# A decoder kernel whose timetable for 884 maxima reckons with VectorE alone, and with VectorE and TensorE together

## The chip, the cores and the metric

The kernel runs on one core of a Trainium2 chip. Its time is the device time of one execution in microseconds (us). The smaller, the better.

## The reference, cut to what matters

A sequence of 1024 tokens with 128 features goes through three parts, each with a residual and a normalisation: four layers of a recurrent cell (sLSTM) with a small gated network behind each, a cross attention with 16 heads over 6404 context rows, and a layer of eight experts.

```python
def step(carry, wx_t):                      # the recurrent cell, 1024 steps, one after the other
    h, c, n, m = carry
    raw = wx_t + jnp.einsum('bhd,hdgo->bhgo', h, rk) + b
    ...
    hn = jax.nn.sigmoid(og) * cn / nn
    return ((hn, cn, nn, mn), hn)
...
scores = jnp.einsum('bqhd,bkhd->bhqk', q, k) * scale
attn = jax.nn.softmax(scores, axis=-1)      # needs the largest score of each query and head
out = jnp.einsum('bhqk,bkhd->bqhd', attn, v).reshape(B, Nq, h * dh)
```

## The kernel before

Each of the four layers is a recurrence over all 1024 tokens. The kernel runs the four as a skewed pipeline, each layer two chunks of 32 tokens behind the one before it: 38 chunks of 32 steps, 1216 steps in all. Each step is a closed ring. TensorE makes 16 small matmuls of the weights with the state (L1179), ScalarE four functions of the gates (L1079 to L1082), VectorE nine small instructions (L1290 to L1319), which end with the new state `st`, and only then can TensorE begin the next step. Beside the ring each chunk has its own work, spread by hand over its 32 steps (`beside`): normalisations, the convolution, the gated network, the gate matmuls for the next chunk. In what follows t is the place of a step in its chunk, 0 to 31.

The first 10 chunks (`chunks(0, FIRST)`) hold nothing else. From chunk 10 on (896 steps, numbered here from 0) part of the attention is laid into the gaps of the ring: 4 blocks of 128 queries with 4 units each (a unit is 4 heads of a block). A unit has 51 tiles of keys, and a unit begins every 52 steps, from step 64 on: in each step three score matmuls (L236 to L238), one value matmul in two passes (L1131) and one exponential on ScalarE (L1068).

The softmax of a unit needs the maxima of its scores beforehand. That is 52 pieces of work for each unit (13 slices of keys for 4 heads), each of one matmul of 128x512 into one of two banks (L245, `pe_max_score`, tile `MB`) and one reduction on VectorE that reads the bank (L253, `dve_max`). They are made during the unit before. With the maxima for one unit more there are 17 sets, 884 pieces. The class `Timetable` sets at build time in which steps they stand. For the maxima of a unit there is a window of 51 steps (fewer for the first two sets); every step in it gets a room, which is `ROOM` (1.15) less the step's entry in `vector_load` less a surcharge for special steps of the attention (`special`), and the 52 pieces are laid out in proportion to the running sum of the rooms. So a step gets none, one or two of them, in rare cases more.

Within a step the order on each engine is fixed. On TensorE: the 16 recurrence matmuls, scores, values, attention work with a bank, the maxima's matmuls, the chunk's matmuls. On VectorE: the nine instructions of the ring, the chunk's work, the attention's, the reductions. All run in that order, so a reduction stands ahead of the next step's L1290.

After step 895 the other 16 units run in a tail without the recurrence, and then the experts; neither is touched.

Of the kernel before, what the change touches and what calls it, by code (L numbers as in the profile page):

```python
# [38 lines left out]
class Attention:  # L39
# [9 lines left out]
    def __init__(self, nc, ctx, dims, blocks_inside):  # L49
        self.nc = nc  # L50
        S, D, HEADS, DHEAD, NK, DC = dims
        self.S, self.D, self.HEADS, self.DHEAD, self.NK, self.DC = dims
        self.TILES = S // P
        self.blocks_inside = blocks_inside
        self.KT = -(-NK // P)
        self.LAST = NK - (self.KT - 1) * P
        self.KEYS = [(i, min(i + 512, NK)) for i in range(0, NK, 512)]
        self.MX = self.HEADS_A_UNIT * len(self.KEYS)
        self.UNITS_A_BLOCK = HEADS // self.HEADS_A_UNIT
        KT, N, U4 = self.KT, self.N, self.UNITS_A_BLOCK  # L60

        def sb(name, shape, dt=F32):
            return ctx.enter_context(nc.sbuf_tensor(name, shape, dt))

        self.identa = sb("identa", [P, P])
        self.keys_h = sb("keys_h", [DC + 1, KT * P], F16)
        self.keys_l = sb("keys_l", [DC, KT * P], F16)
        self.vals = sb("vals", [P, KT, DC + 1])
        self.vals_c = sb("vals_c", [P, KT, 2 * DC + 1], F16)
        self.qk_w = sb("qk_w", [P, HEADS, DC])  # L70
        self.vo_w = sb("vo_w", [DC, HEADS, D])
        self.post_w = sb("post_w", [P, D])
        self.pick_den = sb("pick_den", [DC + 1, 1])
        self.ln_prob = sb("ln_prob", [P, 1])
        self.qh = sb("qh", [DC + 1, U4, N], F16)
        self.ql = sb("ql", [DC, U4, N], F16)
        self.xs = sb("xs", [P, D])
        self.xo = sb("xo", [P, D])
        self.xa = sb("xa", [P, D])
        self.xn_a = sb("xn_a", [P, D])  # L80
        self.xat = sb("xat", [P, P])
        self.sta = sb("sta", [P, 6])
        self.mva = sb("mva", [P, 2])
        self.vra = sb("vra", [P, 1])
        self.rsa = sb("rsa", [P, 1])
        self.neg_half = sb("neg_half", [P, 1])
        self.mx = sb("mx", [P, self.HEADS_A_UNIT, len(self.KEYS)])
        self.mxn = sb("mxn", [P, self.HEADS_A_UNIT])
        self.o_sb = sb("o_sb", [DC + 1, N])
        self.rden = sb("rden", [P, self.HEADS_A_UNIT])  # L90
        self.y_unit = sb("y_unit", [P, blocks_inside * U4 + 1, D])
# [251 lines left out]
class Timetable:  # L343
# [2 lines left out]
    ROOM = 1.15  # L346
    MAX_COST = 0.667

    def __init__(self, at, blocks, steps, chunk_steps, vector_load):
        period, units = at.KT + 1, blocks * at.UNITS_A_BLOCK  # L350
        start = [2 * chunk_steps + period * u for u in range(units + 2)]
        assert start[units] <= steps
        self.units = units
        self.scores = {start[u] + i: (u, i) for u in range(units) for i in range(at.KT)}
        self.values = {s + 1: tile for s, tile in self.scores.items()}
        self.keep = {start[u] + at.KT: u for u in range(units)}
        self.out = {start[u] + period: u for u in range(units - 1)}
        self.block = {24: 0}
        self.block.update({start[at.UNITS_A_BLOCK * b - 2] - 13: b for b in range(1, blocks + 1)})
        self.turn = {s + 9: b for s, b in self.block.items()}  # L360
        self.queries = {35: 0, 46: 1}
        self.queries.update({start[v - 2] - 1: v for v in range(2, units + 2)})
        self.column = {start[v] - 4: v for v in range(units + 1)}
        self.row = {start[v] - 3: v for v in range(units + 1)}
        asked = {v: s for s, v in self.queries.items()}
        special = {s: 1.3 for s in self.out}
        special.update({s: 0.6 for s in self.column})
        for s in self.queries:
            special[s + 2] = special.get(s + 2, 0.0) + 0.7
        for s in self.block:  # L370
            for i in range(9):
                special[s + i] = special.get(s + i, 0.0) + 0.35
        self.maxes = {}
        for v in range(units + 1):
            window = range(max(asked[v] + 2, start[v] - period - 3), start[v] - 4)
            room = [max(0.02, self.ROOM - vector_load[s % chunk_steps] - special.get(s, 0.0)) for s in window]
            total, so_far, n = sum(room), 0.0, 0
            for s, r in zip(window, room):
                so_far += r
                upto = at.MX if s == window[-1] else min(at.MX, int(so_far / total * at.MX + 0.5))  # L380
                if upto > n:
                    self.maxes.setdefault(s, []).extend((v, i) for i in range(n, upto))
                n = upto
        self.uses, free, count = {}, [-1.0, -1.0], [0, 0]

        def take(key, read_at):
            bank = 0 if free[0] <= free[1] else 1
            self.uses[key] = (bank, count[bank])
            free[bank] = read_at
            count[bank] += 1  # L390

        for s in range(steps):
            if s in self.out:
                take(("den", self.out[s]), s + 0.5)
                take(("out", self.out[s]), s + 0.6)
            if s in self.turn:
                take(("turn", self.turn[s]), s + 1.3)
            if s in self.queries:
                take(("queries", self.queries[s]), s + 2.5)
            if s in self.row:  # L400
                take(("row", self.row[s]), s + 1.3)
            for i, key in enumerate(self.maxes.get(s, ())):
                take(("max",) + key, s + 0.7 + 0.01 * i)
        self.block_step = {}
        for s, b in self.block.items():
            for after, step in ((0, 0), (1, 1), (3, 4), (4, 5), (5, 6), (6, 7), (6, 8), (8, 11)):
                self.block_step.setdefault(s + after, []).append((b, step))
        self.scale = {s + 1: (b, 1) for s, b in self.block.items()}
        self.scale.update({s + 6: (b, 2) for s, b in self.block.items()})
        ends = {b: s + 12 for s, b in self.block.items()}  # L410
        self.load = {max(4 * b, -(-ends.get(b - 1, 0) // chunk_steps)): b for b in ends}
        self.store = {ends[b] // chunk_steps: b for b in ends}
        assert len(self.load) == len(self.store) == len(ends)


def slstm_stage(nc, x, w, scratch_in, scratch_out, dims, at, first_row, xa_out):
# [7 lines left out]
    CH = P // L  # L424
# [3 lines left out]
    ITERS = NCH + LAG * (L - 1)  # L428
# [6 lines left out]
    FIRST, KT = 10, at.KT  # L435
# [3 lines left out]
    with ExitStack() as ctx:  # L439
# [530 lines left out]
        def chunks(base, count, plan=None):  # L970


            with nc.Block() as block:
# [217 lines left out]
                def _(dve):  # L1191
# [90 lines left out]
                    for p in range(count):  # L1282
# [44 lines left out]
            nc.gpsimd.sem_clear(range(nums[0], nums[0] + len(nums)))  # L1327
            nc.all_engine_barrier()

        vector_load = [0.4, 0.4, 0.4, 0.4, 0.6, 0.3, 0.6, 0.9, 0, 0.1, 0.4, 0.6, 0.7, 0.7, 0.35, 0.7, 0.1, 0.5, 0.35, 0.32,  # L1330
                       0.5, 0.6, 0.4, 1.2, 1.2, 0.6, 0.6, 0.5, 0.15, 0.15, 0.15, 0.3]
        chunks(0, FIRST)
        chunks(FIRST, ITERS - FIRST, Timetable(at, at.blocks_inside, (ITERS - FIRST) * CH, CH, vector_load))


        with nc.Block() as block:
# [659 lines left out]
```

## Time and profile before

| | |
|---|---|
| runs | 4732.89, 4746.34, 4748.07 us, median 4746.34 |
| profiled execution | 4731.98 us, span of its instructions 4730.3 us |
| busy over the span | PE 82%, PE weight loads 49%, DVE 73%, ACT 62%, POOL 17% |
| recurrence alone (10 chunks) | from 125.3 to 879.4 us |
| recurrence with attention, steps 0 to 895 | from 879.4 to 3239 us |
| attention tail and experts | from 3239 us on |

The profiled execution lies at the low end of the three runs. A time of one step is read as the distance between the starts of its first ScalarE instruction (L1079) and of the next step's.

### The profile page before, as it was taken

What the parts mean: (1) busy time and instruction counts of PE and PEld (TensorE: products, weight loads), DVE (VectorE), ACT (ScalarE), POOL (GpSimd) and SP (SyncE); (2) the same over time, 40 slices, a digit from 0 to 9 for tenths busy, and PEclk for the clock granted to TensorE, in tenths of its full rate; (3) what the DMA queues carried; (4) which work ended last, traced back from release to release, by engine and by line L of the source; (5) the groups of instructions that cost most, each with busy time, mean ns of one, the idle gap of its engine ahead of it and who ended that gap; (6) DMA issues with size and microseconds to landing.
All of it is one profiled execution on the core that took longest, in us unless ns stands there. A gap on an engine that the chain in (4) does not pass through costs nothing. (4 is left out here: it accounts for less than half of the span.)

```text
span 4730.3 us, 104841 instructions
## 1 busy us (share of the span) xinstructions
PE 3893.7 (82%) x38546; PEld 2305.6 (49%) x38546; DVE 3450.6 (73%) x15547; ACT 2928.5 (62%) x9151; POOL 800.6 (17%) x998
## 2 busy tenths in 40 slices
PE   3343434469999999999999999998999999999959
PEld 2332323334454544445444454544666666666636
DVE  4666666788888888888888888886665657666441
ACT  1444444436666666666666666666887878888812
POOL 1000000000000000000000000002554545555500
PEclk7555555559999999999999999998999999999969
DMA  2000000000000000000000000000000000000020
GB/s 61 2 3 3 2 3 2 4 2 2 4 3 3 3 2 4 4 3 2 2 4 3 3 2 3 3 2 3 2 1 3 2 3 2 1 1 1 1 59 5
DMA packets 34825, 26.11 MB, mean 6 GB/s; under 512 B 9453, under 2 KB 32677, under 8 KB 34278
## 3 DMA queue, kind: packets, MB, share of 16 engines
q1 hardware_dynamic: 34310, 19.37, 1.6%
q8 instruction: 308, 5.05, 0.4%
q14 instruction: 207, 1.70, 0.1%
HBM read 15.27 MB, written 2.88 MB: 4 GB/s over the span
## 5 line engine op out<-in xcount | busy, mean ns | idle before, releaser
L1179 PE MATMUL G<-st,rec_w 128*128 128x1 f16 x19456 | 683.1, 165 | 550.2 <-DVE st L1319 532.9
L1179 PEld LDWEIGHTS G<-st,rec_w 128*128 128x128 f16 x19456 | 605.1, 99 | 1006.0 <-DVE st L1319 974.4
L1131 PE MATMUL OA<-pf,vals 128*97 128x512 f32 (+1 forms) x1632 | 849.4, 601 | 0.6
L1500 POOL TENSOR_TENSOR plt<-pft,pht 128x512 f16<-128x512 f32 x544 | 634.9, 1168 | 565.6 <-ACT pft L1495 563.1
L253 DVE TENSOR_REDUCE mx<-MT 128x1 f32<-128x512 f32 x780 | 508.7, 667 | 253.8 <-PE MT L245 248.7
L1088 ACT ACTIVATE st<-hb 32x16 f16<-32x16 f32 x1216 | 259.0, 213 | 696.7 <-DVE hb L1314 696.0
L1493 ACT ACTIVATE pht<-ST,ln_prob 128x512 f16<-128x512 f32 (+1 forms) x816 | 560.5, 687 | 200.4 <-PE ST L238 140.4
L253 DVE TENSOR_REDUCE mx<-MB 128x1 f32<-128x512 f32 (+1 forms) x884 | 571.0, 660 | 41.4 <-PE MB L245 25.9
L1068 ACT ACTIVATE pf<-SC,ln_prob 128x512 f32<-128x512 f32 (+1 forms) x816 | 560.5, 687 | 20.8
L1495 ACT ACTIVATE pft<-ST,ln_prob 128x512 f32<-128x512 f32 (+1 forms) x816 | 554.2, 679 | 0.0
L1079 ACT ACTIVATE tf<-G 32x16 f32<-32x16 f32 x1216 | 211.7, 174 | 483.8 <-PE G L1179 465.4
L1290 DVE SCALAR_TENSOR_TENSOR uu<-tf,cn 32x32 f32<-32x32 f32 x1216 | 214.6, 176 | 295.9 <-ACT tf L1079 287.1
L1561 PE MATMUL OT<-vals_c,pht 128*128 128x193 f16 (+1 forms) x3264 | 409.1, 248 | 7.0 <-DVE o_n L1586 6.4
L245 PE MATMUL MB<-keys_h,qh 96*128 96x512 f16 (+1 forms) x884 | 319.0, 386 | 29.5 <-DVE mx L253 24.5
L1131 PEld LDWEIGHTS OA<-pf,vals 128*97 128x97 f32 (+1 forms) x1632 | 269.3, 167 | 148.3 <-issue 11.7
L1561 PEld LDWEIGHTS OT<-vals_c,pht 128*128 128x128 f16 (+1 forms) x3264 | 288.4, 98 | 98.9 <-issue 17.5
L236 PE MATMUL ST<-qh,keys_l 96*128 96x512 f16 (+1 forms) x816 | 314.3, 385 | 18.9 <-issue 12.2
L1570 PEld LDWEIGHTS OT<-vals_c,plt 128*128 128x128 f16 (+1 forms) x3264 | 228.3, 97 | 202.1 <-issue 13.5
L1296 DVE RECIPROCAL rn<-cn 32x16 f32<-32x16 f32 x1216 | 292.9, 241 | 41.9
L238 PE MATMUL SC<-qh,keys_h 97*128 97x512 f16 (+1 forms) x816 | 314.7, 386 | 0.0
L237 PE MATMUL SC<-ql,keys_h 96*128 96x512 f16 (+1 forms) x816 | 313.0, 384 | 0.0
L238 PE MATMUL ST<-qh,keys_h 97*128 97x512 f16 (+1 forms) x816 | 312.9, 384 | 0.0
(293 smaller groups left out, 6410.4 us busy)
## 6 DMA issues: line engine op xcount, KB each, us to landing
w<-in_L_ffn_W SPq DMA_DIRECT2D x16, 256.0 KB, 5.9
xin<-x SPq DMA_DIRECT2D x38, 48.0 KB, 1.8
rnat<-in_L_attn_rker SPq DMA_DIRECT2D x3, 256.0 KB, 4.2
up_w<-in_L_attn_ff_up SPq DMA_DIRECT2D x1, 672.0 KB
scr_out<-x SPq DMA_DIRECT2D x39, 16.0 KB, 1.6
xin<-scr_in SPq DMA_DIRECT2D x38, 16.0 KB, 1.7
wq_sb<-in_L_xattn_Wq SPq DMA_DIRECT2D x1, 512.0 KB, 3.7
wo_sb<-in_L_xattn_Wo SPq DMA_DIRECT2D x1, 512.0 KB, 8.6
```

Of the source, the lines that this page charges most:

```text
L236: pe.matmul(bank[0:k, :], at.keys_l[:, keys], at.qh[0:DC, unit, :], start=True, stop=False)
L237: pe.matmul(bank[0:k, :], at.keys_h[0:DC, keys], at.ql[:, unit, :], start=False, stop=False)
L238: return pe.matmul(bank[0:k, :], at.keys_h[:, keys], at.qh[:, unit, :], start=False, stop=True)
L245: return pe.matmul(bank[:, 0:a1 - a0], at.qh[0:at.DC, unit, i * P:(i + 1) * P], at.keys_h[0:at.DC, a0:a1], start=True, stop=True)
L253: return at.nc.vector.tensor_reduce(at.mx[:, i, c:c + 1], bank[:, 0:a1 - a0], AX_X, ALU.max)
L1068: s.activation(pf[0:rows, tile % 2, :], SC[tile % 2][0:rows, :], ACT.Exp, scale=1.0 / at.S_SCALE, bias=at.ln_prob[0:rows, 0:1]).then_inc(p ...
L1131: pe.matmul(OA[0:at.DC + 1, :], at.vals[0:rows, i, :], pf[0:rows, tile % 2, :], start=(i == 0), stop=(i == KT - 1)).then_inc(pv_done, 1)
L1179: mm = pe.matmul(g[:, t, c:c + 1], rec_w[:, c, :], st[:, c:c + 1], start=False, stop=(c == C - 1), skip_group_check=True)
L1493: s.activation(ph[0:k, t % NP_, :], SC[t % NS][0:k, :], ACT.Exp, scale=1.0 / at.S_SCALE, bias=at.ln_prob[0:k, 0:1])
L1495: s.activation(pf[0:k, t % NP_, :], SC[t % NS][0:k, :], ACT.Exp, scale=1.0 / at.S_SCALE, bias=at.ln_prob[0:k, 0:1]).then_inc(p_done, 1)
L1500: return eng.tensor_tensor(pl[0:k, t % NP_, :], pf[0:k, t % NP_, :], ph[0:k, t % NP_, :], ALU.subtract)
L1561: pe.matmul(OA[i // 2][:, (i % 2) * 256:(i % 2) * 256 + VC], ph[0:k, t % NP_, i * P:(i + 1) * P], at.vals_c[0:k, j, :], start=(j == 0 and ...
```

## The change

The room of a step is now reduced by a second list too, `tensor_load`, with an entry for each t at which the chunk has matmuls. The entries of `vector_load` at several of those t become smaller, and the least room is 0 instead of 0.02.

```diff
@@ -346,7 +346,7 @@
-    def __init__(self, at, blocks, steps, chunk_steps, vector_load):
+    def __init__(self, at, blocks, steps, chunk_steps, vector_load, tensor_load):
@@ -373,7 +373,8 @@
-            room = [max(0.02, self.ROOM - vector_load[s % chunk_steps] - special.get(s, 0.0)) for s in window]
+            room = [max(0.0, self.ROOM - vector_load[s % chunk_steps] - tensor_load[s % chunk_steps] - special.get(s, 0.0))
+                    for s in window]
@@ -1327,10 +1328,12 @@
-        vector_load = [0.4, 0.4, 0.4, 0.4, 0.6, 0.3, 0.6, 0.9, 0, 0.1, 0.4, 0.6, 0.7, 0.7, 0.35, 0.7, 0.1, 0.5, 0.35, 0.32,
...
+        tensor_load = [0, 0, 0, 0, 0, 0, 0, 0, 0, 0.4, 0.7, 0, 0, 0.3, 0, 0, 0.5, 0.6, 0, 0,
...
```

No instruction is added or removed, 884 pieces stay 884; only their steps change. From step 64 to 891 there are 828 pieces in both kernels. Before, 133 of these 828 steps hold two of them and 133 none; now 170 hold two or more (two of these hold three, steps 328 and 744) and 172 none. By t the number of steps with two or more, and with none, in these 828 steps:

| t | two or more: before, now | none: before, now |
|---|---|---|
| 0 | 7, 5 | 3, 3 |
| 1 | 4, 10 | 2, 4 |
| 2 | 4, 12 | 2, 0 |
| 3 | 4, 8 | 0, 0 |
| 5 | 6, 16 | 2, 0 |
| 7 | 0, 0 | 11, 14 |
| 8 | 15, 22 | 4, 4 |
| 9 | 18, 10 | 2, 2 |
| 10 | 1, 0 | 0, 4 |
| 13 | 0, 0 | 8, 23 |
| 14 | 4, 16 | 0, 0 |
| 16 | 9, 4 | 4, 4 |
| 18 | 11, 4 | 0, 0 |
| 19 | 4, 19 | 0, 0 |
| 26 | 0, 0 | 0, 17 |
| 28 | 15, 10 | 3, 3 |
| 29 | 8, 7 | 2, 2 |
| 30 | 19, 20 | 0, 0 |

The other places change by two steps or less in either column.

Three places show the moves. First VectorE in step 173 (t = 13) and step 174 (t = 14), before: from the reduction of step 173 (`mx`) over the nine instructions of the ring and one of the chunk's (`gq`) to the reduction of step 174.

```order
L253 TENSOR_REDUCE mx<-MB 128x1
L1290 SCALAR_TENSOR_TENSOR uu<-tf,cn 32x32
L1293 SCALAR_TENSOR_TENSOR cn<-ei,uu 32x16
L1296 RECIPROCAL rn<-cn 32x16
L1298 SCALAR_TENSOR_TENSOR vv<-ei,tz 32x16
L1302 SCALAR_TENSOR_TENSOR ww<-to,rn 32x16
L1312 TENSOR_TENSOR cn<-uu,vv 32x16
L1314 SCALAR_TENSOR_TENSOR hb<-ww,cn 32x16
L1316 SCALAR_TENSOR_TENSOR st<-ww,cn 32x16
L1319 TENSOR_TENSOR st<-hb,st 32x16
L886 SCALAR_TENSOR_TENSOR gq<-gq,TP 128x168
L253 TENSOR_REDUCE mx<-MB 128x1
```

The same place now, from the chunk's last work of step 173 on (line numbers behind the diff are one higher).

```order
L887 SCALAR_TENSOR_TENSOR gq<-gq,gs 128x168 x2
L1291 SCALAR_TENSOR_TENSOR uu<-tf,cn 32x32
L1294 SCALAR_TENSOR_TENSOR cn<-ei,uu 32x16
L1297 RECIPROCAL rn<-cn 32x16
L1299 SCALAR_TENSOR_TENSOR vv<-ei,tz 32x16
L1303 SCALAR_TENSOR_TENSOR ww<-to,rn 32x16
L1313 TENSOR_TENSOR cn<-uu,vv 32x16
L1315 SCALAR_TENSOR_TENSOR hb<-ww,cn 32x16
L1317 SCALAR_TENSOR_TENSOR st<-ww,cn 32x16
L1320 TENSOR_TENSOR st<-hb,st 32x16
L887 SCALAR_TENSOR_TENSOR gq<-gq,TP 128x168
L253 TENSOR_REDUCE mx<-MB 128x1 x2
```

The reduction of step 173 has gone behind that of step 174: t = 13 has none, t = 14 has two, and L1291 of step 175 stands behind both.

Second VectorE in step 179 (t = 19), before: from the ring's last instruction over two of the chunk's small ones (`pw`, `ke`) and the reduction to the start of step 180.

```order
L1319 TENSOR_TENSOR st<-hb,st 32x16
L1258 TENSOR_SCALAR pw<-nlo 32x16
L1260 TENSOR_SCALAR ke<-nlo 32x16
L253 TENSOR_REDUCE mx<-MB 128x1
L1290 SCALAR_TENSOR_TENSOR uu<-tf,cn 32x32
L1293 SCALAR_TENSOR_TENSOR cn<-ei,uu 32x16
```

The same place now.

```order
L1320 TENSOR_TENSOR st<-hb,st 32x16
L1259 TENSOR_SCALAR pw<-nlo 32x16
L1261 TENSOR_SCALAR ke<-nlo 32x16
L253 TENSOR_REDUCE mx<-MB 128x1 x2
L1291 SCALAR_TENSOR_TENSOR uu<-tf,cn 32x32
L1294 SCALAR_TENSOR_TENSOR cn<-ei,uu 32x16
```

One reduction has become two in this step; step 178 has one instead of two.

Third TensorE in step 186 (t = 26), before: recurrence, scores, values, a maximum's matmul (`MB`), and three gate matmuls of the chunk.

```order
L1179 MATMUL G<-st,rec_w 128x1 x16
L236 MATMUL SC<-qh,keys_l 128x512
L237 MATMUL SC<-ql,keys_h 128x512
L238 MATMUL SC<-qh,keys_h 128x512
L1131 MATMUL OA<-pf,vals 97x512
L245 MATMUL MB<-keys_h,qh 128x512
L828 MATMUL G<-gx,gate_w 128x32 x3
```

The same place now.

```order
L1180 MATMUL G<-st,rec_w 128x1 x16
L236 MATMUL SC<-qh,keys_l 128x512
L237 MATMUL SC<-ql,keys_h 128x512
L238 MATMUL SC<-qh,keys_h 128x512
L1132 MATMUL OA<-pf,vals 97x512
L829 MATMUL G<-gx,gate_w 128x32 x3
```

The maximum's matmul is gone from this step, and with it the reduction on VectorE.

## Rows read from the trace of the kernel before

The columns of Rows 1 are: window, its length, busy time of each engine with the number of its instructions, the granted TensorE clock as a share of 2.4 GHz, the DMA share. Step numbers and t are as above.

**Rows 1.** Windows: steps 32 to 63; steps 64 on; two unit boundaries.
```profile
core 0: us, PE busy (x) PEld busy (x) DVE busy (x) ACT busy (x) POOL busy (x), PEclk, DMA share, GB/s
954.70:1061.60 106.90, 63.35 (x664) 36.20 (x665) 86.97 (x396) 34.82 (x177) 3.44 (x10) 0.50 0.01 3
1061.60:3239.30 2177.70, 2070.41 (x20303) 1062.64 (x20302) 1871.10 (x9692) 1434.26 (x5325) 96.08 (x276) 0.98 0.01 3
1330.70:1346.00 15.30, 15.03 (x117) 9.20 (x116) 9.34 (x49) 7.63 (x28) 1.11 (x4) 0.67 0.00 1
2425.50:2438.30 12.80, 12.34 (x116) 6.79 (x115) 9.27 (x48) 7.55 (x27) 1.11 (x4) 0.87 0.01 1
```

**Rows 2.** Groups by shape, 1061.6 to 3239.3 us: busy us, mean ns, idle before.
```profile
L253 DVE TENSOR_REDUCE mx<-MB 128x1 f32<-128x512 f32 x764 | 509.8, 680 | 35.5 <-PE MB L245 21.5
...
L245 PE MATMUL MB<-keys_h,qh 96*128 96x512 f16 x764 | 271.5, 380 | 3.9 <-DVE mx L253 3.9
```

**Rows 3.** Timeline of an ordinary step, all engines: start us, length us, instruction.
```profile
1904.97 0.17 ACT L1079 ACTIVATE tf<-G 32x16 f32<-32x16 f32 x1
...
1906.25 0.38 PE L245 MATMUL MB<-keys_h,qh 96*128 96x512 f16 x1
...
1906.43 0.17 DVE L1319 TENSOR_TENSOR st<-hb,st 32x16 f16<-32x16 f32 x1
...
1906.66 0.55 PE L1179 MATMUL G<-st,rec_w 128*128 128x1 f16 x16
1906.91 0.69 DVE L253 TENSOR_REDUCE mx<-MB 128x1 f32<-128x512 f32 x1
...
1907.30 0.17 ACT L1079 ACTIVATE tf<-G 32x16 f32<-32x16 f32 x1
...
1907.52 0.17 DVE L1290 SCALAR_TENSOR_TENSOR uu<-tf,cn 32x32 f32<-32x32 f32 x1
```

**Rows 4.** ScalarE timeline, first instruction of steps 110, 111, 112.
```profile
1177.97 0.17 ACT L1079 ACTIVATE tf<-G 32x16 f32<-32x16 f32 x1
...
1180.63 0.17 ACT L1079 ACTIVATE tf<-G 32x16 f32<-32x16 f32 x1
...
1182.95 0.17 ACT L1079 ACTIVATE tf<-G 32x16 f32<-32x16 f32 x1
```

**Rows 5.** The same of steps 142, 143, 144.
```profile
1266.10 0.17 ACT L1079 ACTIVATE tf<-G 32x16 f32<-32x16 f32 x1
...
1268.42 0.17 ACT L1079 ACTIVATE tf<-G 32x16 f32<-32x16 f32 x1
...
1271.31 0.17 ACT L1079 ACTIVATE tf<-G 32x16 f32<-32x16 f32 x1
```

**Rows 6.** The same of steps 147 and 148.
```profile
1279.06 0.17 ACT L1079 ACTIVATE tf<-G 32x16 f32<-32x16 f32 x1
...
1281.87 0.17 ACT L1079 ACTIVATE tf<-G 32x16 f32<-32x16 f32 x1
```

**Rows 7.** The same of steps 358 and 359.
```profile
1832.41 0.17 ACT L1079 ACTIVATE tf<-G 32x16 f32<-32x16 f32 x1
...
1835.24 0.17 ACT L1079 ACTIVATE tf<-G 32x16 f32<-32x16 f32 x1
```

**Rows 8.** The same of steps 92 and 93.
```profile
1132.25 0.17 ACT L1079 ACTIVATE tf<-G 32x16 f32<-32x16 f32 x1 [0.23 <-PE G L1179]
...
1135.18 0.17 ACT L1079 ACTIVATE tf<-G 32x16 f32<-32x16 f32 x1 [0.63 <-PE G L1179]
```

**Rows 9.** The same of steps 316 and 317.
```profile
1720.90 0.17 ACT L1079 ACTIVATE tf<-G 32x16 f32<-32x16 f32 x1 [0.23 <-PE G L1179]
...
1723.61 0.17 ACT L1079 ACTIVATE tf<-G 32x16 f32<-32x16 f32 x1 [0.42 <-PE G L1179]
```

**Rows 10.** Timeline of step 122 (t = 26), VectorE and TensorE.
```profile
1215.46 0.16 DVE L1319 TENSOR_TENSOR st<-hb,st 32x16 f16<-32x16 f32 x1
...
1215.73 0.54 PE L1179 MATMUL G<-st,rec_w 128*128 128x1 f16 x16
```

More of the change, by code:

```diff
@@ L1328, in chunks @@
             nc.all_engine_barrier()
-        vector_load = [0.4, 0.4, 0.4, 0.4, 0.6, 0.3, 0.6, 0.9, 0, 0.1, 0.4, 0.6, 0.7, 0.7, 0.35, 0.7, 0.1, 0.5, 0.35, 0.32,
-                       0.5, 0.6, 0.4, 1.2, 1.2, 0.6, 0.6, 0.5, 0.15, 0.15, 0.15, 0.3]
+        vector_load = [0.4, 0.4, 0.4, 0.4, 0.6, 0.3, 0.6, 0.9, 0, 0, 0, 0.6, 0.7, 0.7, 0.35, 0.7, 0, 0.16, 0.35, 0.32,
+                       0.5, 0.6, 0.32, 1.2, 1.2, 0.6, 0.5, 0.35, 0, 0, 0, 0.2]
+        tensor_load = [0, 0, 0, 0, 0, 0, 0, 0, 0, 0.4, 0.7, 0, 0, 0.3, 0, 0, 0.5, 0.6, 0, 0,
+                       0, 0, 0.3, 0, 0, 0, 0.35, 0.35, 0.4, 0.35, 0.35, 0.25]
         chunks(0, FIRST)
-        chunks(FIRST, ITERS - FIRST, Timetable(at, at.blocks_inside, (ITERS - FIRST) * CH, CH, vector_load))
+        chunks(FIRST, ITERS - FIRST, Timetable(at, at.blocks_inside, (ITERS - FIRST) * CH, CH, vector_load, tensor_load))
         with nc.Block() as block:
```

## The prediction

> **What bounds the kernel now.** I read the windows by stage first. From step 64 to the end of the recurrence there are 2177.7 us for 832 steps, 2.62 us each, with TensorE busy for 2070 us (95%), VectorE for 1871 us (86%) and ScalarE for 1434 us (66%) [rows 1]. This is the stretch in which most maxima move; 52 of the 884 pieces are made in steps 32 to 63, of 106.9 us [rows 1]. Before step 32, in the tail and in the experts nothing changes.
>
> A busy share does not tell what a step costs, since the step is a ring. So I took the timeline of one plain step, 385 [rows 3]. It goes from 1904.97 to 1907.30, 2.33 us. At 1906.25 the matmul of its one maximum starts (0.38 us, so until 1906.63); at 1906.43 VectorE starts the last instruction of the ring, until 1906.60; at 1906.66 TensorE begins the next recurrence. Both inputs of that start, the engine and the state, are there within 0.03 us of each other. Behind the ring VectorE then runs the reduction, 1906.91 to 1907.60, and the next step's L1290 starts at 1907.52, when its input from ScalarE (1907.30 + 0.17) has just come. So one maximum in a plain step is free on both engines. Step 111 with one maximum reads 2.32 us too [rows 4], and I found no step of this stretch below that.
>
> What a second maximum costs has two parts that fall on different steps. Its matmul stands ahead of the next recurrence in its own step. Its reduction stands ahead of the next step's L1290, so it lengthens the **next** step. Each counts only as far as its engine is the later one: the two lengthen a step by the greater, not by the sum.
>
> **Prices, by pairs of equal places in the trace of before.** The distance of the first ScalarE instructions of two steps is the length of a step; n is the number of maxima.
> - VectorE, behind a step with two, place lightly loaded: step 147 follows one with two and takes 1281.87 - 1279.06 = 2.81 us [rows 6], against 2.32: +0.49. Step 359 begins 2.83 us after 358, which follows a pair at t = 5 [rows 7]: +0.51. Step 143 follows a pair at t = 14: 1271.31 - 1268.42 = 2.89, against step 111 behind a single: 1182.95 - 1180.63 = 2.32 [rows 4, 5]: +0.57.
> - At t = 1, 2, 3 the chunk's own VectorE work already fills the step; there nothing is free and I take 0.60 for a further reduction, near its whole length, 0.68 us [rows 2].
> - VectorE, behind a step with none: step 142 (none before it, two in it) takes 1268.42 - 1266.10 = 2.32 us, step 110 (one, one) 1180.63 - 1177.97 = 2.66 [rows 4, 5]: -0.34 for t = 14.
> - TensorE: step 92 (t = 28) with two takes 1135.18 - 1132.25 = 2.93 us [rows 8], step 316 with one 1723.61 - 1720.90 = 2.71 [rows 9]: 0.22 for a maximum in a step that TensorE fills. In step 142 two maxima in a plain step cost nothing at all, so there TensorE has this 0.22 to spare.
> - t = 26, the place with the most removals: VectorE's last ring instruction ends at 1215.46 + 0.16 = 1215.62, the recurrence starts at 1215.73 [rows 10], 0.11 us later, against 0.06 in the plain step (1906.66 - 1906.60 [rows 3]). So VectorE is only about 0.05 us behind TensorE. Taking TensorE's 0.22 away gives 0.05, because the step then waits for VectorE.
>
> **The sum, steps 64 to 891,** with the counts of the table of places:
> - more steps with two: t = 1, 2, 3: +18 at 0.60 = +10.8; t = 5: +10 at 0.51 = +5.1; t = 14: +12 at 0.57 = +6.8; t = 19: +15 at 0.49 = +7.4; t = 20, 21, 25: +5 at 0.5 = +2.5; t = 8: +7. The step behind it (t = 9) had a pair in front in 15 cases already and is partly filled by TensorE; between 0 and 0.5 I take 0.25, the middle, = +1.8. Sum +34.4.
> - fewer steps with two: t = 18: -7 at 0.49 = -3.4; t = 0: -2 at 0.60 = -1.2; t = 28 and 29: -6 at 0.22 = -1.3; t = 22: -2 at 0.4 = -0.8. t = 9 and 16, -13: the steps behind (t = 10, 17) have chunk matmuls and are filled by TensorE anyway, so 0. Sum -6.7.
> - more steps with none: t = 13: +15 at -0.34 = -5.1; t = 26: +17 at -0.05 = -0.9; t = 7: +3 at about -0.45 = -1.4; t = 10 and 17, where TensorE is the later: +6 at -0.22 = -1.3. Those at other places that lose or gain one nearly cancel: 0. Sum -8.7.
> - special steps and steps 32 to 63 (step 47 goes from one to three, step 48 from two to none), and the third maximum in steps 328 and 744: between -3 and +4, taken as +1.
>
> Together 34.4 - 6.7 - 8.7 + 1 = **+20 us**, all from VectorE. The bounds: with every added pair at 0.4 and the removals at full TensorE price (t = 26: -3.7) it is +9; with every added pair at the whole reduction, 0.68, it is +31. The sum stands against the profiled execution, 4731.98 us, and gives 4752. That execution lies 14 us (0.3%) below the median of the runs, 4746.34; I put the same 20 us on the median: 4766, and say **4765 us**, +0.4%. A difference under 0.3% (14 us) can't be told from no change here: the runs shown spread over 15.
>
> **A rule against a row.** In this stretch TensorE's matmul time fills 95% [rows 1], which would make it the engine to relieve. The weight loads fill 1062.6 of 2177.7 us, 49%, and VectorE 86% [rows 1]. The Trainium skill (Perfetto Trace Analysis, Identifying the Most-Contended Engine) says that matmul busy time is not a good measure and that one goes by weight loads on Tensor and by occupancy elsewhere, and relieves the fullest engine first. By that rule VectorE is the one, and a change that makes pairs of reductions to spare TensorE goes the wrong way; by matmul busy time it would go the right way, which is the first rival. The sum above needs neither.
>
> **Rivals.**
> 1. *TensorE is the later one nearly everywhere, faster.* For it: 95% busy, and in the plain step its matmul ends 0.03 us behind VectorE's state. Then added reductions are hidden and each maximum that leaves a step with chunk matmuls gives 0.22. From t = 9, 10, 13, 16, 17, 22 and 26 to 31 together 68 leave (t = 26 alone 17): -15 us, 4731. It decides if the steps behind the new pairs stay at 2.3 to 2.4. Against it: steps 143, 147 and 358 [rows 5, 6, 7], the very pairs that become many. Chance 0.05.
> 2. *The added pairs cost about half,* because a step that is late on VectorE catches up in the next, or the special steps gain: +9, 4755, within 0.3%. For it: the last reduction of each row of 13 is shorter, and unit boundaries lose some maxima right ahead of their long VectorE work (steps 167, 425, 583 and 841). Against it: the lengths read above are from start to start, so a catching up would show in them; step 142 and the steps after it are not shorter than 2.32. Chance 0.20.
> 3. *The clock.* The two unit boundaries of the same steps (168 and 584) take 15.3 us at a mean clock of 0.67 and 12.8 us at 0.87 [rows 1]: 2.5 us for some 7 us more at the lower level, 1.2 GHz. 12 of 15 boundaries have such a stretch. If the steps without maxima bring one to each boundary and to as many places again, that is 15 x 2.5 = +38 on top, 4785 or more; if they only shift, +-6. Against it: at t = 26 and 13 TensorE keeps over 80% of its work. The Trainium skill (TensorE: Matmul & The Clock Gate, Part 1) says that idleness of TensorE lowers the clock and activity restores it; here the row agrees so far that the lower level stands at the boundaries, where no scores run. Chance 0.04.
> 4. *The change doesn't do what it says.* In part it doesn't: steps at t = 28 to 30 with two go from 42 to 37 only. As the numbers are laid out in proportion, a lower room for a few places raises the share of all others. If the moves cancel throughout: 4746. Chance 0.03.
>
> **Chances and range.** Forecast (+14 us or more) 0.68, its own range 4757 to 4778; rivals as above. Slower by over 0.3%: 0.68 + 0.04 = 0.72. Within: 0.20 + 0.03 = 0.23. Faster: 0.05. The range must take in the half price (4755), the upper bound of the sum (+31, 4777) and that the runs themselves lie between 4733 and 4748: 4747 to 4781.
>
> **What would show it.** In the profile after: the stretch from step 64 to 895 takes 2197 instead of 2177.7 us; steps behind a pair at t = 2, 5, 14, 19 read 2.8 to 3.1 us; steps at t = 14 behind none read 2.32; steps at t = 26 without a maximum 2.63 instead of 2.68 (2.46 would speak for rival 1); L1079's idle time behind TensorE changes little, and that of L1179 behind `st` grows by about the 20 us. I am wrong if the steps behind the new pairs don't grow, if the price at t = 26 is 0.2, or if the boundaries change by more than 5 us together.

## The result and the profile after

The changed kernel takes 4756.56 us in the median of 14 runs (4752.18 to 4758.34), the kernel before 4746.51 us in the median of 14 runs (4731.36 to 4756.77). The medians stand 10 us apart. The ratio is 1.0024, 95% interval 1.0015 to 1.0034: slower by 11 us, 7 to 16. That interval covers the scatter of the runs, not the clock's part between two programs, which the last experiment puts at some 10 us; that the change itself costs time rests on the steps, read below. The direction is the forecast's, the size about half of it, and below the 14 us that the prediction called the least to be told apart. The profiled execution took 4758.22 us, its span is 4756.5 us, 26.2 more than before. The pages of both read alike; here the page of the kernel after.

```profile
span 4756.5 us, 104841 instructions
...
PE 3902.9 (82%) x38546; PEld 2310.9 (49%) x38546; DVE 3450.4 (73%) x15547; ACT 2928.4 (62%) x9151; POOL 800.6 (17%) x998
```

No engine has more or less to do. The windows of the kernel after for steps 32 to 63, for steps 64 on, and for the seven steps 270 to 276 around a unit boundary (columns as in [rows 1]):

```profile
core 0: us, PE busy (x) PEld busy (x) DVE busy (x) ACT busy (x) POOL busy (x), PEclk, DMA share, GB/s
955.30:1061.20 105.90, 63.03 (x664) 36.02 (x665) 87.02 (x396) 34.84 (x178) 3.44 (x10) 0.50 0.01 3
1061.20:3262.20 2201.00, 2079.07 (x20303) 1068.14 (x20302) 1871.22 (x9692) 1434.20 (x5325) 96.32 (x276) 0.98 0.01 3
1604.80:1628.30 23.50, 22.53 (x193) 11.78 (x192) 16.84 (x85) 12.98 (x48) 0.08 (x1) 0.78 0.04 10
```

Steps 64 on take 23.3 us more than in [rows 1], steps 32 to 63 1.0 less. The same seven steps in the kernel before:

```profile
1602.80:1621.60 18.80, 17.98 (x191) 9.94 (x190) 15.76 (x84) 12.94 (x47) 0.06 (x1) 1.00 0.05 13
```

They took 4.7 us less there, at a full clock; after, the mean clock is 0.78. So part of the 23 us is the clock and not the timetable. To separate the two I added up, in both profiles, the lengths of the same 655 steps away from the unit boundaries (of steps 64 to 891 all but those from three before a unit's start to seven behind it; a length is again the distance of two first ScalarE instructions). No half clock stands in them in either profile, and the 349 of them whose own and preceding number of maxima are the same differ by 0.2 us in sum. They take **11.4 us** more. The boundary steps take 12.0 us more, of which 2.7 stand in steps whose own or preceding number changed; the rest, 9.3, is mainly clock: 12 of the 15 boundaries had a stretch at half clock before, 78 us in all, and all 15 have one after, 99 us. (Among the boundary steps at full clock in both profiles, the changed ones take 2.1 us more and the others 0.4.) The tail, where nothing changed, took 3.2 us more, and the start of step 0 was 0.6 later. So 11.4 + 2.7 - 1.0 = 13.1 us belong to the places, and 9.3 + 3.2 + 0.6 = 13.1 to this pair of executions.

Where they stand is seen step by step. Steps 173, 174, 175 of the place shown first in the change (ScalarE's timeline after, first instruction of steps 174, 175, 176; those of before are shown with the last experiment):

```profile
1353.22 0.17 ACT L1080 ACTIVATE tf<-G 32x16 f32<-32x16 f32 x1
...
1355.54 0.17 ACT L1080 ACTIVATE tf<-G 32x16 f32<-32x16 f32 x1
...
1358.43 0.17 ACT L1080 ACTIVATE tf<-G 32x16 f32<-32x16 f32 x1
```

Step 174, with two maxima and none before it, takes 2.32 us (before 2.66), step 175 behind the pair 2.89 (before 2.32). Step 180, behind the new pair at t = 19 (steps 180 and 181 start at):

```profile
1368.47 0.17 ACT L1080 ACTIVATE tf<-G 32x16 f32<-32x16 f32 x1
...
1371.00 0.17 ACT L1080 ACTIVATE tf<-G 32x16 f32<-32x16 f32 x1
```

2.53 us instead of 2.32. One reduction of this pair is short: the last slice of each head has 260 columns, and its reduction takes 416 ns instead of 680 (kernel before, group by shape):

```profile
L253 DVE TENSOR_REDUCE mx<-MB 128x1 f32<-128x260 f32 x64 | 26.6, 416 | 0.5
```

Of the 13 steps away from the boundaries that stand behind a new pair at t = 19, the nine with two full reductions in front grew by 0.48 us each, the four with a short one by 0.21; together 5.1 us. And step 186 (t = 26), which has lost its maximum (steps 186 and 187 start at):

```profile
1382.78 0.17 ACT L1080 ACTIVATE tf<-G 32x16 f32<-32x16 f32 x1
...
1385.46 0.17 ACT L1080 ACTIVATE tf<-G 32x16 f32<-32x16 f32 x1
```

2.68 us, as long as before. TensorE has less to do and nothing is gained. The groups by shape say the same of the whole stretch; first after, then the kernel before:

```profile
L253 DVE TENSOR_REDUCE mx<-MB 128x1 f32<-128x512 f32 x764 | 507.9, 680 | 35.0 <-PE MB L245 20.6
L1180 PE MATMUL G<-st,rec_w 128*128 128x1 f16 x13296 | 457.7, 164 | 106.4 <-DVE st L1320 95.9
```

```profile
L1179 PE MATMUL G<-st,rec_w 128*128 128x1 f16 x13296 | 457.5, 164 | 92.7 <-DVE st L1319 79.6
```

TensorE's wait for the new state ahead of its recurrence has grown from 79.6 to 95.9 us.

One place has a price that the prediction did not have. Three steps before a unit's start, TensorE also writes the row of maxima (L263) into one of the two banks, so a second maximum in that step is the third use of two banks. Step 425 in the kernel before, with two maxima:

```profile
2007.80 0.39 PE L245 MATMUL MB<-keys_h,qh 96*128 96x512 f16 x1
...
2008.22 0.69 DVE L253 TENSOR_REDUCE mx<-MB 128x1 f32<-128x512 f32 x1 [1.15 <-PE MB L245]
...
2008.97 0.39 PE L245 MATMUL MB<-keys_h,qh 96*128 96x512 f16 x1 [0.79 <-DVE mx L253]
```

The second matmul waits until the first reduction has freed its bank, and the next recurrence stands behind it. The step takes 4.43 us with two maxima and 3.26 with one (after). The same 1.18 us are lost or gained wherever the count of such a step went between one and two: steps 425, 477 and 841 lost their second maximum, 165 and 581 got one.

### The profile page after: what moved, and what is told of

It reads as the page before. It is cut to its first block and busy times, and to the rows that moved or that the text cites. A ratio compares the mean times of both kernels' runs of the same rounds, so it can differ in the third digit from the quotient of the medians.

```text
span 4756.5 us, 104841 instructions
## 1 busy us (share of the span) xinstructions
PE 3902.9 (82%) x38546; PEld 2310.9 (49%) x38546; DVE 3450.4 (73%) x15547; ACT 2928.4 (62%) x9151; POOL 800.6 (17%) x998
## 3 DMA queue, kind: packets, MB, share of 16 engines
HBM read 15.27 MB, written 2.88 MB: 4 GB/s over the span
## 5 line engine op out<-in xcount | busy, mean ns | idle before, releaser
L1291 DVE SCALAR_TENSOR_TENSOR uu<-tf,cn 32x32 f32<-32x32 f32 x1216 | 214.6, 177 | 316.2 <-ACT tf L1080 308.6
```

## The experiments

The theory: a pair of maxima costs by VectorE in the next step, unless TensorE's chunk matmuls fill that step anyway. Rival A: TensorE is the later engine, its relief is what counts. Rival B: the difference of the two kernels comes from the clock at the unit boundaries. The table gives the ratio to the kernel before in runs on the same chip, and the difference to the profile of before: in the 655 steps away from the boundaries, in steps 32 to 63, and in the boundary steps whose own or preceding number of maxima changed and that stand at full clock in both profiles. The last three columns together are what the places cost.

| kernel | ratio, 95% interval | 655 steps, us | steps 32 to 63, us | changed boundary steps, us |
|---|---|---|---|---|
| the change | 1.0024 (1.0015 to 1.0034) | +11.4 | -1.0 | +2.1 |
| e1_vector_list_alone | 0.9992 (0.9983 to 1.0001) | -7.0 | +2.7 | -0.9 |
| e2_tensor_list_alone | 1.0072 (1.0058 to 1.0086) | +29.7 | +2.5 | +7.3 |
| e3_short_reduce_before | 0.9835 (0.9822 to 0.9848) | -60.7 | -11.2 | none changed |
| e4_short_reduce_after | 0.9814 (0.9801 to 0.9827) | -6.3 to e3 | -0.8 to e3 | -2.2 to e3 |
| e5_priced | 0.9942 (0.9927 to 0.9957) | -21.5 | -1.9 | +1.5 |
| e6_fill_before | 1.0000 (0.9989 to 1.0011) | -0.1 | 0.0 | none changed |
| e7_fill_after | 1.0046 (1.0030 to 1.0062) | +11.4 to e6 | -1.0 to e6 | +3.0 to e6 |
| e8_fill_out_only_before | 0.9993 (0.9982 to 1.0005) | +0.1 | 0.0 | none changed |
| e9_max_room | 1.0008 (0.9997 to 1.0018) | +6.9 | +1.0 | +2.0 |
| e10_only_13_to_14 | 0.9984 (0.9973 to 0.9996) | +2.5 | 0.0 | +0.2 |

**The two halves of the change.** First the new list for VectorE alone:

```diff
-        tensor_load = [0, 0, 0, 0, 0, 0, 0, 0, 0, 0.4, 0.7, 0, 0, 0.3, 0, 0, 0.5, 0.6, 0, 0,
-                       0, 0, 0.3, 0, 0, 0, 0.35, 0.35, 0.4, 0.35, 0.35, 0.25]
+        tensor_load = [0] * 32
```

> The new vector_load, tensor_load all zeros. The smaller entries stand at steps with chunk matmuls, so pairs gather there: 160 steps of two (133 before), with t = 9, 10, 16, 17 at 21, 12, 15, 13 (before 18, 1, 9, 0), t = 0 to 5 at 11 (before 25), t = 18 at 0 (before 11), and t = 7, 12 without a maximum in 19 and 13 (before 11, 8). Price theory (a pair costs 0.5 to 0.6 us where VectorE is the later engine in the next step, 0 to 0.25 where TensorE fills it): -14 x 0.6 - 11 x 0.49 for pairs gone, +11 x 0.22 (t = 10), +13 x 0.5 (t = 17), +6 x 0.45 (t = 27), +10 x 0.22 (t = 29 to 31), +4 x 0.4 (t = 22), zeros at t = 7, 12, 13, 11, 15 -7.5: about -5 us against the kernel before, in any case at or below it. Rival (TensorE is the later engine, so pairs in steps with chunk matmuls are what costs): slower than before by some 10 us.

Measured 4737.93 us against 4741.58, -4 us, an interval that just takes in no change; in its places -7.0, +2.7 and -0.9, together -5.2, as forecast. Then the new list for TensorE with the old one for VectorE:

```diff
-        vector_load = [0.4, 0.4, 0.4, 0.4, 0.6, 0.3, 0.6, 0.9, 0, 0, 0, 0.6, 0.7, 0.7, 0.35, 0.7, 0, 0.16, 0.35, 0.32,
-                       0.5, 0.6, 0.32, 1.2, 1.2, 0.6, 0.5, 0.35, 0, 0, 0, 0.2]
+        vector_load = [0.4, 0.4, 0.4, 0.4, 0.6, 0.3, 0.6, 0.9, 0, 0.1, 0.4, 0.6, 0.7, 0.7, 0.35, 0.7, 0.1, 0.5, 0.35, 0.32,
+                       0.5, 0.6, 0.4, 1.2, 1.2, 0.6, 0.6, 0.5, 0.15, 0.15, 0.15, 0.3]
```

> The old vector_load with the new tensor_load: the same idea, stronger. 202 steps of two or more (8 of them three and more), 54 of them at t = 0 to 4 (before 19), t = 5: 17 (6), t = 6: 5 (0), t = 20: 15 (0); t = 28 to 30 20 (42); none at t = 10, 13, 17, 26, 27 in 22, 21, 24, 19, 7 steps (0, 8, 4, 0, 2). Price theory: pairs at t = 0 to 4 +35 x 0.57, t = 5 and 6 +8.5, t = 11 +3, t = 14 +6, t = 18 to 20 +16, threes +5; TensorE relief -22 x 0.22 - 22 x 0.22 - 20 x 0.19 - 13 x 0.3 - 2: about +37 us against before, clearly slower than the change. Rival (TensorE the later one): about 100 maxima away from chunk matmuls at 0.22: 20 us faster than before.

4775.45 against 4741.58 us, +34; in its places +39.5 where +37 was forecast. The loss of the change sits in its TensorE list. Its VectorE list alone gives a little back by the places; the runs alone don't show that. Rival A had both signs wrong.

**VectorE's price taken away.** In both timetables the reductions of 16 of the 17 sets read 64 columns:

```diff
-    return at.nc.vector.tensor_reduce(at.mx[:, i, c:c + 1], bank[:, 0:a1 - a0], AX_X, ALU.max)
+    return at.nc.vector.tensor_reduce(at.mx[:, i, c:c + 1], bank[:, 0:columns or a1 - a0], AX_X, ALU.max)
...
-                            dve_max(at, MB[bank], i).then_inc(mb_read[bank], 1)
+                            dve_max(at, MB[bank], i, 64 if u < plan.units else None).then_inc(mb_read[bank], 1)
```

> The timetable of before; the reductions of the 16 sets for units beside the recurrence read 64 columns of the bank instead of 512, so those maxima are over part of the scores. Takes most of VectorE's price away and leaves TensorE's. Price theory: all single maxima that cost 0.1 to 0.47 at t = 2 to 8, 11 to 15 become free (some 2.3 us a chunk, 60 us), the 60 pairs outside TensorE's steps lose 0.5 each (30 us), unit boundaries some 10: about -100 us. Rival (TensorE the later one nearly everywhere): less than -30 us.

> The changed timetable with the same short reductions (maxima of the same 16 sets over part of the scores). Read against e3_short_reduce_before. Price theory: with VectorE's price gone only TensorE's terms are left, t = 26 now at its full 0.22 (-17 x 0.22), t = 28, 29 (-6 x 0.22), t = 10, 17 (-6 x 0.22): about -6 us against it, where the same two timetables with full reductions stand +13 us apart by their places. Rivals: if the difference of the two kernels came from the clock or from bank waits it stays at +10 or more.

4661.26 and 4653.52 us: -80 us to the kernel before (the expectation's 100 was too much: 60.7 and 11.2 us stand in the 655 steps and in steps 32 to 63, and the boundaries gave 2 in all instead of some 10), and the changed timetable is now the **faster** one by 8 us, where its slowest run (4653.95) lies below e3's fastest (4659.27). A short reduction takes 215 ns (group of e3, by shape) and not 680:

```profile
L253 DVE TENSOR_REDUCE mx<-MB 128x1 f32<-128x64 f32 x776 | 162.6, 215 | 41.3 <-PE MB L245 23.9
```

The windows from step 64 on, e3 and then e4:

```profile
1049.80:3164.70 2114.90, 2067.53 (x20303) 1065.50 (x20302) 1560.28 (x9692) 1437.00 (x5325) 96.02 (x276) 0.98 0.01 3
```

```profile
1049.80:3158.80 2109.00, 2058.59 (x20303) 1064.16 (x20301) 1558.91 (x9692) 1434.22 (x5324) 96.02 (x276) 0.98 0.01 3
```

And step 186 (t = 26), in e3 with its maximum and in e4 without (first instructions of steps 186 and 187):

```profile
1357.21 0.17 ACT L1079 ACTIVATE tf<-G 32x16 f32<-32x16 f32 x1
...
1359.88 0.18 ACT L1079 ACTIVATE tf<-G 32x16 f32<-32x16 f32 x1 [0.37 <-PE G L1179]
```

```profile
1356.63 0.17 ACT L1080 ACTIVATE tf<-G 32x16 f32<-32x16 f32 x1
...
1359.08 0.17 ACT L1080 ACTIVATE tf<-G 32x16 f32<-32x16 f32 x1
```

2.67 us with it, 2.45 without: the 0.22 us of TensorE are there, and with full reductions VectorE hides them. Away from the boundaries 11 steps at t = 26 lost their maximum and got no pair in front; they take 0.22 us less each here, and 0.00 less with full reductions. This pair settles the cause: same moves, opposite sign (-9.3 us in the places against +12.5), and only the length of the reduction differs. It speaks against rival B as well, since no half clock stands in the 655 steps.

**A timetable by prices.** The lengths of steps before give each t a price for its first and its second maximum; the 52 cheapest offers of a window are taken.

```diff
+            prices = []
+            for s in window:
+                first, second = first_price[s % chunk_steps], second_price[s % chunk_steps]
+                more = min(0.66, special.get(s, 0.0))
+                prices += [(first + more, s), (max(first, second) + more, s), (0.7 + more, s)]
...
+            chosen = sorted(s for _, s in sorted(prices)[:at.MX])
...
+        first_price = [0.01, 0.01, 0.1, 0.14, 0.25, 0, 0.2, 0.47, 0.08, 0, 0.22, 0.25, 0.34, 0.33, 0, 0.14, 0, 0.17, 0, 0,
+                       0.12, 0, 0, 0.6, 0.6, 0, 0, 0.2, 0.22, 0.22, 0.22, 0.3]
+        second_price = [0.6, 0.6, 0.6, 0.6, 0.6, 0.5, 0.6, 0.66, 0.2, 0.03, 0.23, 0.66, 0.66, 0.66, 0.56, 0.66, 0.05, 0.5, 0.45, 0.45,
+                         0.6, 0.5, 0.41, 0.66, 0.66, 0.6, 0.5, 0.45, 0.22, 0.22, 0.22, 0.4]
```

> A timetable by the measured prices: each step of a window offers a first and a second maximum at a price by t (first_price, second_price, read from the lengths of steps before; a surcharge for special steps as before), and the 52 cheapest offers are taken. Pairs at t = 0 to 5: 0 (before 25), t = 14, 18, 19: 6 (19), t = 8, 9, 16: 68 (42), t = 10: 26 (1), t = 28 to 30: 64 (42); none at t = 7, 12, 13 in 26, 20, 16 steps (11, 8, 8). Price theory, against before: -25 x 0.57 - 4 x 0.55 - 9 x 0.45 for dear pairs gone, +25 x 0.23 (t = 10) + 22 x 0.22 (t = 28 to 30) + 3 for other pairs, -15 x 0.47 - 12 x 0.34 - 8 x 0.33 - 2 for the maxima taken away: about -22 us, 0.5% faster than before. Rival (the later engine is TensorE; room by both loads together is right): it has more pairs in TensorE's steps than any kernel so far and should be slower than before by 10 us or more.

4716.41 us against 4744.26: ratio 0.9942, -28 us, faster than both kernels. In its places -21.5, -1.9 and +1.5: -22 as forecast. From step 64 on:

```profile
1060.80:3219.50 2158.70, 2073.08 (x20303) 1062.65 (x20301) 1872.62 (x9692) 1436.97 (x5324) 96.84 (x276) 0.98 0.01 3
```

Steps 200 to 202 (t = 8, 9, 10) in it, and then in the kernel before (first instructions of steps 200 to 203). The priced one has 0, 2, 2 and 2 maxima in steps 199 to 202, the other 1, 1, 2 and 1.

```profile
1414.07 0.17 ACT L1082 ACTIVATE tf<-G 32x16 f32<-32x16 f32 x1
...
1416.39 0.17 ACT L1082 ACTIVATE tf<-G 32x16 f32<-32x16 f32 x1
...
1419.08 0.17 ACT L1082 ACTIVATE tf<-G 32x16 f32<-32x16 f32 x1
...
1422.07 0.17 ACT L1082 ACTIVATE tf<-G 32x16 f32<-32x16 f32 x1 [0.38 <-PE G L1182]
```

```profile
1419.04 0.17 ACT L1079 ACTIVATE tf<-G 32x16 f32<-32x16 f32 x1
...
1421.84 0.17 ACT L1079 ACTIVATE tf<-G 32x16 f32<-32x16 f32 x1
...
1424.24 0.17 ACT L1079 ACTIVATE tf<-G 32x16 f32<-32x16 f32 x1
...
1427.08 0.17 ACT L1079 ACTIVATE tf<-G 32x16 f32<-32x16 f32 x1 [0.25 <-PE G L1179]
```

2.32, 2.69 and 2.99 us against 2.80, 2.40 and 2.84. The three steps take 8.00 against 8.04 us, though the four hold one maximum more: leaving t = 7 empty gives 0.48 in step 200, and the two pairs more cost 0.29 and 0.15.

**Greater load in place of the sum.**

```diff
-            room = [max(0.0, self.ROOM - vector_load[s % chunk_steps] - tensor_load[s % chunk_steps] - special.get(s, 0.0))
+            room = [max(0.0, self.ROOM - max(vector_load[s % chunk_steps], tensor_load[s % chunk_steps]) - special.get(s, 0.0))
```

> The change with one word other: room = 1.15 - max(vector_load, tensor_load) - special instead of the sum of both. Asks if it is the adding of the loads that costs. 142 steps of two (change 170). Pairs against before: t = 1 to 3 +11, t = 19, 20, 22 +19, t = 25 to 27 +13, t = 31 +13, t = 28 to 30 -23, t = 9 and 16 -15 (free ones), t = 0 and 18 -7. Price theory: +6 for t = 1 to 3, +9 for 19 to 22, +6 for 25 to 27, +4 for t = 31, -5 for 28 to 30, -4 for 0 and 18, +1 for t = 7, -2 for 10 and 17: about +16 us against before in its places, no better than the change, since any room by load moves pairs away from TensorE's steps where they are cheap. Rival (the adding is the fault, the greater load would be right): same as before or faster.

4746.35 against 4744.19 us, no difference to be measured in the runs; +6.9, +1.0 and +2.0 in its places, together +9.9, where I had expected +16. The change has +12.5 by the same count (13.1 with the boundary steps at half clock). So by the places the greater load still loses most of what the sum loses, and the adding is the smaller part of the fault. Some of the gap to the forecast is that 15 of its new pairs away from the boundaries hold a short reduction; the rest was not followed up.

**The clock at the unit boundaries.** Four matmuls more in the first score step of each unit and in its last step:

```diff
+                    def fill(bank, u):
+                        for _ in range(4):
+                            pe.matmul(bank[:, :], at.keys_l[:, 0:P], at.qh[0:at.DC, u % at.UNITS_A_BLOCK, :], start=True, stop=True)
...
+                        if i == 0 and u:
+                            fill(SC[tile % 2], u)
...
+                            if plan and n in plan.keep:
+                                tile = (plan.keep[n] + 1) * KT
+                                pe.wait_ge(p_done, tile - 1)
+                                fill(SC[tile % 2], plan.keep[n])
```

> The kernel before with four idle matmuls of 128x512 more (results overwritten) in the first score step of each unit from the second on and in the last step of each unit, which has no scores. Asks for the clock: the half clock stands at these unit boundaries (78 us in all, 12 of 15 boundaries in the profile of before). If TensorE's want of work there lowers the clock, the filling keeps it up: -28 us for the clock (2.5 us for 7), +19 for the matmuls themselves (0.87 us each in the last step, half hidden in the first): about -9 us. If the filling does not reach the clock: +19 us and the same stretches at half clock.

> The changed kernel with the same filling. Against e6_fill_before: if part of what the two profiles differ by (26 us) is the clock at the boundaries and the filling steadies it, only the places' price is left, +13 us. If the filling does not reach the clock: between +5 and +26, as the clock falls.

> The kernel before with the four matmuls only in the first score step of a unit. The first half-clock instructions stand there or one to two steps behind it. If that is late enough to hold the clock: -28 + 6 = some -20 us; if the want of work lies before it (score tiles of four rows and the last step): about +6 us with the half-clock stretches as before.

The filling reaches the clock: in e6 4 boundaries have half-clock stretches, 24 us in all, not 12 with 78. The granted clock of the runs agrees, 0.8745 in the median of e6's 12 and 0.867 in that of 24 runs of the kernel before. In e8 there are 8 with 68 us, so the matmuls of the first score step alone do little for the clock: neither of e8's two expectations came true. Steps 166 to 171 (a boundary), the kernel before and then e6:

```profile
1327.90:1348.00 20.10, 19.78 (x159) 11.30 (x158) 13.73 (x72) 11.82 (x42) 1.29 (x5) 0.75 0.00 1
```

```profile
1328.60:1347.10 18.50, 17.25 (x168) 9.38 (x167) 13.85 (x72) 11.85 (x43) 1.27 (x5) 1.00 0.01 1
```

1.6 us less with eight matmuls more. Over all it balances, where -9 had been expected: e6 4744.58 us against 4744.26; the interval of e8 (4740.61) takes in no change too. e6 ran 71 us less at half clock than the kernel before; at 0.39 us each (worked out with the last experiment) that is the forecast 28 us, so by this estimate the matmuls took about 28 and not 19. e7, the change with the same filling, took 4770.20 us, 26 more than e6 and not 13. In its profile the 655 steps are again 11.4 us above e6, exactly as in the unfilled pair, and the boundary steps 12.7; one boundary, around step 636, had 20.5 us at half clock in a row and alone was 9.5 us longer. e8 had the same 20.5 us at the same steps. In the runs e7 stood 30 us longer at half clock than e6 (granted clock 0.872 and 0.8745), about 12 us by the same estimate, which with the 13 of the places gives the 26. So the places' price came out clean and equal twice, but the filling did not make the two kernels' clocks equal, and why that stretch is so long stays open.

**One kind of move alone.**

```diff
+        for s in range(2 * chunk_steps + 13, steps, chunk_steps):
+            moved = self.maxes.get(s, [])
+            if len(moved) == 1 and len(self.maxes.get(s + 1, [])) == 1 and moved[0][0] == self.maxes[s + 1][0][0]:
+                self.maxes[s + 1] = self.maxes.pop(s) + self.maxes[s + 1]
```

> The kernel before with one kind of move alone: 18 single maxima of t = 13 go into the next step, which then holds two. Price theory: the step at t = 14 loses 0.34, the one at t = 15 gains 0.57, two of the moves stand at a unit boundary and count nothing: 16 x 0.23 = +4 us, in the profile at t = 15 +9 and at t = 14 -5, t = 13 unchanged. Rival (TensorE the later one; t = 13 has a chunk matmul): -18 x 0.22 = -4 us, at t = 13.

Starts of steps 173 to 176, the kernel before, then e10:

```profile
1350.59 0.17 ACT L1079 ACTIVATE tf<-G 32x16 f32<-32x16 f32 x1
...
1353.25 0.17 ACT L1079 ACTIVATE tf<-G 32x16 f32<-32x16 f32 x1
...
1355.91 0.17 ACT L1079 ACTIVATE tf<-G 32x16 f32<-32x16 f32 x1
...
1358.23 0.17 ACT L1079 ACTIVATE tf<-G 32x16 f32<-32x16 f32 x1
```

```profile
1350.32 0.18 ACT L1083 ACTIVATE tf<-G 32x16 f32<-32x16 f32 x1
...
1352.97 0.17 ACT L1083 ACTIVATE tf<-G 32x16 f32<-32x16 f32 x1
...
1355.30 0.17 ACT L1083 ACTIVATE tf<-G 32x16 f32<-32x16 f32 x1
...
1358.17 0.17 ACT L1083 ACTIVATE tf<-G 32x16 f32<-32x16 f32 x1
```

2.66, 2.66, 2.32 us before; 2.65, 2.33, 2.87 in e10. Summed away from the boundaries: t = 13 0.0, t = 14 -3.6, t = 15 +6.3, all other t within 0.2: +2.5 us, of the +4 expected. (14 of the 18 moves stand away from the boundaries; 8 of them cost 0.56 at t = 15, and 6 that hold a short reduction 0.30.) The steps do what the theory says. But the runs say 4737.48 against 4744.19 us, -7 us, and no step that the move touches is behind that.

The granted clock of the runs is. It has a median of 0.870 in e10 and 0.867 in the 23 runs of the kernel before beside it. Twice the missing share times the run's time is the time at half clock: 1232 and 1262 us, 30 less. Over those 23 runs of one and the same kernel the time rises by 0.36 us for each us at half clock (correlation 0.94; over the 24 runs beside e6 0.39 and 0.93). So the clock is worth about -11 us and the places +3, an estimate of -8, where -7 was measured. The runs alone don't tell a difference of a few us in the timetable; read beside their clocks they fit the places in this case and in e7.

## Why the prediction was right, and where its sizes were off

- *The mechanism* (the pair's reduction stands ahead of the next step's L1290): right. Steps 174, 175 and 180 read about as forecast, e3 and e4 turn the sign round with the reduction's length alone, e10 shows one kind of move by itself.
- *The prices* held away from the boundaries. Steps behind a new pair of full reductions grew by 0.51 us at t = 6 (8 steps; taken 0.51), by 0.56 at t = 15 (6 steps; 0.57), by 0.60 at t = 3 and 4 (0.60) and by 0.48 at t = 20 (9 steps; 0.49). At t = 9 it was 0.24 to 0.28 in 7 steps; there the 0.25 was only the middle of a range, so that hit is luck.
- *What was mis-sized, away from the boundaries:* the prediction's own terms for these 655 steps add up to +13.1 (53 of the 67 added pairs 26.7, the removals -6.5 and -7.1); 11.4 was measured. All added pairs were priced as full reductions. Ten at t = 2, 3 and 19 hold a short one and cost 0.21 to 0.46 instead of 0.49 to 0.60, 2.6 us less in all.
- *What was mis-sized, elsewhere:* for the boundary steps and steps 32 to 63 the same terms give +6.9 (14 added pairs 7.7, removals -1.8, special steps +1); 1.7 was measured. The added pairs did cost there: 0.47 to 0.60 in the six steps at full clock behind a full new pair with nothing special around it (175, 226, 484, 591, 642, 692). What the sum lacked is the wait for a bank three steps before a unit's start. Three such steps lost their second maximum (-3.5 us, booked at -0.2) and two got one (+2.4, booked at +1.0). Steps 32 to 63 gave -1.0, and the term for special steps had been +1. The two account for 4 of the 5 us; the last was not followed up.
- *t = 26*: right. Taking away the maximum gave 0.00 in the step itself (2.68 us both; the same in all 11 steps away from the boundaries that got no pair in front) and 0.04 each in the steps behind. That was the place where a count of TensorE's work alone would have booked 17 x 0.22.
- *Rival 1* fell: at t = 26 TensorE's relief shows only in e4. The Trainium skill's rule of the fullest engine (Perfetto Trace Analysis, Identifying the Most-Contended Engine), by which VectorE and not TensorE was the one to relieve, agrees: shorter reductions gave 80 us. *Rival 2*, half the size, is what the runs gave, and two of its grounds held: the short last reduction of each row, and steps 425 and 841, which it named, with 1.18 us each. Its other ground, that a late step catches up in the next, did not: the steps behind the pairs were as long as priced. By chances, "within 0.3%" had 0.23, and the ratio of 0.24% lies there; too much stood on the full size, whose own range, 4757 to 4778, the measured 4756.56 just misses. That the wide range, 4747 to 4781, holds it says little about the size.
- *Rival 3*, the clock: it was in the profile (9.3 us at the boundaries) but not in the runs' medians to that extent. The before profile was a lucky one (4731.98 in a spread of 4731 to 4757), and the profiled pair, 26 us apart, overstates the change twofold. I added the same 20 us to the median as to the profile; that the two kernels' runs would stand at about the same clock was assumed and not shown beforehand, and e10 and e7 show that it can shift a median by 10 us either way. The prediction put the lower clock where no scores run. In fact TensorE is not idle there: its matmuls fill 19.78 of 20.1 us in steps 166 to 171.
- *Rival 4*, the change doing little of what it says: steps with chunk matmuls did lose 68 maxima on balance; the moves as such did not cancel.
- *The signs it named:* L1179's wait behind `st` was to grow by about the 20 us and grew by 16, from 79.6 to 95.9; L1079's behind TensorE, said to change little, grew from 139.6 to 148.3. The stretch was to take 2197 us and took 2201.0, but 9 us of the 23 are the clock's, so that this comes so close is luck. Steps at t = 26 were to read 2.63 and read 2.68. One sign of being wrong did come: the boundaries changed by 12.0 us together in the profiles, over the 5 allowed. Of these 2.7 lie with the timetable and 9.3 with the clock, so it does not touch the mechanism.

## What to carry to other kernels

In a ring of steps that two engines share, a piece of work laid into the gaps costs by the engine that is later at that point, and each engine's part may fall on another step. Here hand-made lists of loads, one engine's, both added or the greater of both, came out between 5 us better and 40 us worse by the places. Read the price of one more and of one fewer piece at each place from pairs of equal places in one trace, look at the places with a third user of two buffers by themselves, and give the work to the cheapest: that made 28 us here. And before a few microseconds are believed from runs, or from two profiles, compare the same steps one by one, leave out those in which the clock differs, and compare the granted clocks of the runs.

## What the runs showed of the hardware

- Away from the boundaries steps with the same work around them mostly repeat to 0.01 or 0.02 us over 2 ms and between programs (2.32, 2.66 and 2.88 us in three kernels), so a profile tells a change of 3 us in 2180 that the runs' median told with the wrong sign.
- At a unit boundary TensorE's granted clock falls to 1.2 GHz for 3 to 10 us, although the engine is busy there for nearly the whole time (19.78 of 20.1 us in steps 166 to 171). The low clock itself makes matmuls longer, so the stretch ahead of the fall says more: in the 5 us before it matmuls filled all of the time at the fall in step 479, still at 2.4 GHz, and between 72% and 99% of it at the other 11 boundaries of the kernel before that had one.

```profile
2147.20:2152.20 5.00, 5.00 (x46) 3.43 (x46) 3.32 (x20) 3.21 (x11) 0.00 (x0) 1.00 0.01 2
```

- What TensorE runs at these boundaries, beside the usual tiles, are score tiles of four rows, values of four rows and matmuls of one or 128 columns. With eight matmuls of 128x512 more, 4 of 15 boundaries had such a stretch instead of 12. The Trainium skill (TensorE: Matmul & The Clock Gate, Part 1) ties the lower clock to an idle engine; the fall in step 479 does not fit that, since the profile shows no gap ahead of it. What it is about this work that lets the clock fall is not shown. The mean clock, 0.98 over the stretch in either kernel, hides all this.
- What half clock costs this kernel: 0.36 to 0.39 us for each us at 1.2 GHz, over 23 and 24 runs of the kernel before.
- A VectorE maximum over one bank takes 215 ns for 64 columns (e3), 416 ns for 260 and 680 ns for 512 (before), by the groups by shape.
